# Two-level attention and a mixture of experts on one core: six of sixteen token tiles go to the experts by slots instead of through all eight

## The reference

```python
x = x + attention(layernorm(x))     # 16 heads of 8; window of 64 keys and four levels of pooled keys
h = layernorm(x)
gate = softmax(h @ Wg.T)            # 8 experts
val, idx = top_k(gate, 2); val /= val.sum() + 1e-9
for e in range(8):                  # 512 hidden columns: a, b = 256 each
    a, b = split(h @ W1[e].T + b1[e])
    out += ((a * sigmoid(b)) @ Wo.T + bo) * comb[..., e]
x = x + out
```

## Time and profile before

| | us |
|---|---|
| median of 3 runs | 288.18 |
| lowest and highest | 287.26, 295.06 |
| the profiled execution | 288.01 |
| its span | 286.2 |

### The profile page before, as it was taken

How to read it: one execution, slowest core, us unless ns; L and a number is a source line. 1 busy time by engine, 2 the same in 40 slices (tenths; PEclk the granted TensorE clock), 3 DMA queues, 4 the chain that set the end, 5 groups by cost and what they waited for, 6 DMA issues and landing times.

```text
span 286.2 us, 7298 instructions
## 1 busy us (share of the span) xinstructions
PE 273.4 (96%) x2705; PEld 226.5 (79%) x2705; DVE 154.6 (54%) x453; ACT 154.7 (54%) x316; POOL 135.8 (47%) x235
## 2 busy tenths in 40 slices
PE   7999999999999999993999999999999999999994
PEld 6868767887788988883888888788888678888883
DVE  7782644633344001322643162789886987777773
ACT  6765745534653432742487456544676555555551
POOL 7753302300041154140171301888885678888881
PEclk9999999989999975998999799999999999999999
DMA  7221176340097687558445011300000000000000
GB/s 212 61 58 60 57 171 192 81 126 2 11 289 277 168 229 170 145 155 165 128 144 154 26 22 21 85 10 10 10 11 9 10 11 10 9 11 18 11 9 19
DMA packets 19683, 24.14 MB, mean 84 GB/s; under 512 B 8312, under 2 KB 14456, under 8 KB 19648
## 3 DMA queue, kind: packets, MB, share of 16 engines
q1 hardware_dynamic: 18528, 22.80, 28.8%
q10 hardware_dynamic: 1120, 0.89, 1.2%
HBM read 11.91 MB, written 5.37 MB: 60 GB/s over the span
## 4 chain that ended last, share of the span: by engine, by line
PE 88%; DVE 3%; issue 3%; DMA 2%; SPq 1%; ACT 1%; POOL 1%; DVEq 0%; ACTq 0%; POOLq 0%
PE bank L1327 13%; PE bank L1140 12%; PE bank L1142 11%; PE bank L1141 11%; PE bank L1303 8%; PE bank L1306 6%; PE bank L1289 5%; PE bank L1221 3%; PE bank L1150 3%; PE bank L1331 2%; PE bank L1271 2%; PE bank L1237 2%; PE bank L1183 1%; DMA qst<-nshiftT 1%; PE bank L1171 1%
## 5 line engine op out<-in xcount | busy, mean ns | idle before, releaser
L752 POOL TENSOR_TENSOR work<-work 128x256 f32<-128x256 f32 x110 | 81.4, 744 | 31.2 <-DVE work L1123 18.3
L1123 DVE SCALAR_TENSOR_TENSOR work<-bank,comb,work 128x256 f32<-128x256 f32 x128 | 58.9, 480 | 24.7 <-ACT work L893 23.4
L893 ACT ACTIVATE work<-bank 128x256 f32<-128x256 f32 x128 | 48.4, 384 | 42.8 <-PE bank L1142 40.3
L868 ACT ACTIVATE work<-bank 128x512 f32<-128x512 f32 x64 | 37.7, 594 | 44.0 <-PE bank L1306 39.8
L1327 PE MATMUL bank<-work,vaug 128*64 128x64 f32 x1024 | 45.7, 235 | 0.0
L1327 PEld LDWEIGHTS bank<-work,vaug 128*64 128x64 f32 x1024 | 37.0, 144 | 9.0 <-issue 1.6
L658 POOL COPY vaug<-vwin 128x64 f32<-128x64 f32 x64 | 13.2, 250 | 51.7 <-PE bank L1331 51.5
L1303 PE MATMUL bank<-bar,ident_r 128*128 128x512 f32 x64 | 34.1, 533 | 0.0
L1306 PEld LDWEIGHTS bank<-qmk,kst 98*128 98x128 f32 x128 | 26.4, 206 | 4.3 <-issue 1.0
L1306 PE MATMUL bank<-qmk,kst 98*128 98x256 f32 x128 | 27.3, 297 | 0.0
L1141 PE MATMUL bank<-arena,xT_hi 128*128 128x512 f32 x64 | 25.1, 392 | 0.0
(11 more groups left out here) (217 smaller groups left out, 532.4 us busy)
## 6 DMA issues: line engine op xcount, KB each, us to landing
w_stage<-w SPq DMA_DIRECT2D x8, 512.0 KB, 3.9
qmk<-qst SPq DMA_DIRECT2D x20, 96.0 KB
qst<-arena SPq DMA_DIRECT2D x12, 128.0 KB, 3.8
kst<-arena SPq DMA_DIRECT2D x9, 128.0 KB, 3.2
qst<-q_rows SPq DMA_DIRECT2D x3, 384.0 KB, 4.2
qmk<-q_rows SPq DMA_DIRECT2D x12, 96.0 KB
p_rows<-kpool SPq DMA_DIRECT2D x2, 512.0 KB, 4.5
attT<-denom SPq DMA_DIRECT2D x8, 128.0 KB, 2.8
```

The lines of the kernel that those rows point to most:

```text
L752: gp.tensor_tensor(gacc[t % 2][:, :], gacc[t % 2][:, :], gtmp[(adds - 1) % TMP_RING][:, :], ALU.add).then_inc(acc_done, 1)
L868: act.activation(prob[lo % P_RING][:, :, :, :], bank[sc % SCORE_BANKS][:, :].rearrange("p (c j q) -> p c j q", c=2, j=GH), ACT.Exp).then_i ...
L893: act.activation(sig[hn % SIG_RING][:, :], bank[hn % HID_BANKS][:, HID:2 * HID], ACT.Sigmoid).then_inc(sig_done, 1)
L1123: dve.scalar_tensor_tensor(dst[:, :], bank[hn % HID_BANKS][:, 0:HID], comb[:, t, e:e + 1], sig[hn % SIG_RING][:, :], ALU.mult, ALU.mult).t ...
```

## The change

Tiles 0 and 1 of batch 0 and all of batch 1 keep all eight experts. Tiles 2 to 7 of batch 0 are routed. A step `rank` counts with small matmuls of the picks (against ones and a matrix of earlier tokens) how many picks of an expert stand before each token, and `route` makes from it, on DVE, for each token and each of its two picks the row of a slot (`slot_of`), and for each of 19 slot tiles of 128 rows the expert it belongs to (`expert_of`). Experts begin at multiples of 128 rows, which is why 12 x 128 picks take 19 tiles. POOL scatters the normalised rows to DRAM with 12 indirect DMAs in three steps, SP reads them back in five loads, PE transposes them (`slotsT`) and makes one unit of hidden work a slot, with the weights at an offset that is read into a register (`value_load`). The high parts of W1 are first moved side by side into `whi` by six DMAs. DVE multiplies without the gate value, SP writes the 128x256 results to DRAM, and POOL gathers two rows a token with two indirect DMAs a tile (`pull`); `hidT` of a routed tile is four matmuls against diagonal matrices of the gate values (`diag`), which add and transpose at once. For this the second norm and gate of batch 0 stand earlier, gate part 2 at the end of unit 6, and those of batch 1 stand beside the slots. SP also writes zeros to the slot rows at the start.

The core of the diff:

```diff
+DENSE = 2
+ROUTED = T // P - DENSE
+SLOT_TILES = (ROUTED * P * TOPK + E * (P - 1)) // P
...
-        5: {0: [("rden", 0)], 6: [("spread", 0, 0)], 7: [("spread", 0, 1), ("proj", 0, 0)], 8: [("proj", 0, 1)], 9: [("stat2", 0, 0)]},
+        4: {9: [("rden", 0)]},
+        5: {3: [("spread", 0, 0), ("spread", 0, 1), ("proj", 0, 0)], 4: [("proj", 0, 1)], 5: [("stat2", 0, 0)], 6: [("stat2", 0, 1)],
...
+        7: {0: [("rank",), ("route",)], 1: [("scatter", 0)], 3: [("gate", 0, 3), ("weigh",)], 4: [("scatter", 1)], 8: [("scatter", 2)]},
...
+        (0, 4): [("rden", 1)], (1, 5): [("hidT", 0)], (1, 6): [("spread", 1, 0), ("spread", 1, 1)], (1, 7): [("y", 0), ("proj", 1, 0)],
+        ("slot", 0): [("proj", 1, 1), ("stat2", 1, 0)], ("slot", 2): [("hidT", 1), ("stat2", 1, 1)], ("slot", 4): [("y", 1), ("apply2", 1, 0)],
...
+        ("slot", 15): [("gate", 1, 1)], ("slot", 17): [("gate", 1, 2), ("diag",)], ("slot", 18): [("gate", 1, 3)],
...
+            if e == 0 and r < TT:
+                s.append(("pull", r))
...
+                if u == NG:
+                    spill_reciprocals(0)
+                    load_reciprocals(0)
+                if u == UNITS - 1:
+                    sp.wait_ge(score_full, u * SPU)
+                    for n in range(6):
+                        sp.wait_ge(w1_ready, n + 1)
+                        move(whi[:, n, :], w1T_hi[n]).then_inc(whi_in, 16)
...
+            spill_reciprocals(1)
+            sp.wait_ge(slots_sent, 16 * TOPK * ROUTED)
+            sp.wait_ge(vaug_ready, 2 * UNITS)
+            for q in range(SLOT_GROUPS):
+                sp.dma_start(slot_rows[q], slots_dram[4 * q * P:min(4 * q + 4, SLOT_TILES) * P, :].rearrange("(i p) c -> p i c", p=P))\
+                  .then_inc(slots_in[q], 16)
             load_reciprocals(1)
...
+                    for n in range(*SCATTERS[step[1]:step[1] + 2]):
+                        r, k = n // TOPK, n % TOPK
+                        gp.indirect_dma_start(slots_dram, bass.IndirectOffsetOnAxis(ap=slot_of[:, k, r:r + 1], axis=0),
+                                              xnorm[:, DENSE + r, :], None).then_inc(slots_sent, 16)
...
+                    if r == 0:
+                        for i in range(OUT_RING):
+                            gp.wait_ge(hidden_sent[i], 16 * len(range(i, SLOT_TILES, OUT_RING)))
...
+                    for k in range(TOPK):
+                        gp.indirect_dma_start(pulled[r % 2][k], None, hidden_dram,
+                                              bass.IndirectOffsetOnAxis(ap=slot_of[:, k, r:r + 1], axis=0)).then_inc(pulled_in[r % 2], 16)
...
+                    pe.wait_ge(hid_done, hn - HID_BANKS + 1)
...
+                    mine = pe.value_load(expert_of[0:1, i:i + 1], min_val=0, max_val=E - 1)
+                    hi, lo = (w[:, bass.ds(mine, 1), :].rearrange("p o n -> p (o n)") for w in (whi, w1T_lo))
+                    ins = split3(bank[hn % HID_BANKS][:, :], tuple(x[i // 4][:, i % 4 * P:(i % 4 + 1) * P] for x in slotsT), (hi, lo))
```

256 lines of the change are left out of this document (205 added, 51 removed).

## The result

| | before | after |
|---|---|---|
| median of 4 runs each, side by side | 291.0 us | 317.92 us |
| lowest and highest | 287.26, 295.06 | 315.25, 328.25 |

The changed kernel takes 1.102 times as long (95% interval 1.083 to 1.121). That ratio, like those further down, is of the faster executions of each kernel, those that the clock slowed least; the quotient of the two medians is 1.092. The changed kernel is slower by 27 us, where 4.4 us less was forecast, and lies outside the range. Its profiled execution is the slowest of the four, 328.25 us (span 326.4).

What follows compares the result with a forecast made beforehand. PE was taken to set the experts' pace, with POOL 0.3 us a tile away. Terms -20.0 + 4.7 + 0.8 + 4.1 + 3.0 + 3.0 = -4.4 took 288.0 to 283.6 us; range 272 to 299.

Steps and rivals of the forecast that it cites:

- Units removed: Tiles 2 to 7 of batch 0: 19 slots replace 48 units, -20.0 us on PE, all on the chain.
- matmuls added: PE: slot transposes 2.1, six hidT steps 1.3 and rank's 12 small matmuls 1.3, together +4.7 us.
- Zeros, the six moves of W1 and earlier steps of batch 0: Start and attention stage: cost 0, the 4.58 us hole at batch 0's projection staying, give or take 1.
- Unit 7: End of attention: PE waits 0.8 us at rank; values behind scatters cost nothing at 0.75 us an issue, +3.4 at 1.28.
- g: Time one indirect DMA of 128 rows holds POOL: taken as 0.75 us, bounds 0.33 and 1.28.
- Reciprocals of batch 1: First projection of batch 1: their read lands late behind slot-row loads, a hole of +4.1 us (3.0 to 5.8).
- The slot stage: 19 slots beside batch 1's norm and gate: DVE sets the pace, 23.1 us against PE's 19.1, net +3.0.
- Register loads: Before each slot PE reads the expert's number: taken as 0; serial-loads rival 291 to 303 us, chance 0.17.
- Pulls: Tiles 8 to 13: two gathers a tile on POOL, 57.5 us against PE's 53.8, +3.0 after the ring's slack.
- POOL becomes the bound: Slower rival, six tiles with gathers: at 1.28 us an issue pulls cost 9.4, result 294.4 us, chance 0.25.
- DVE idle in a third of the experts' stage: Argument for the faster rival: DVE now idles 0.2 us before each multiply in the experts' stage.
- the covers: Faster rival: early reciprocals, PE's bank slack and short POOL issues hide most costs; -13.5, 274.5 us, chance 0.22.

Runs made afterwards that it cites:

- moves only: Kernel before with only batch 0's moved steps and two w1 steps placed as in the changed kernel, no routing; median 296.92 us beside 287.69.
- W1 first: Changed kernel with the last two W1 steps at the first place of unit 7, ahead of the scatters in POOL's order; median 326.46 us.
- constant expert: Routed kernel with reordered steps and idle matmuls, each slot's expert fixed at build, no register loads; median 311.85 us, 319.89 with loads.
- changed kernel again: Changed kernel rerun unedited for a second profile; median 328.39 us beside 287.69 of the kernel before.
- fillers: Changed kernel with idle TensorE matmuls ahead of four waits (both projections, rank, slot 0); median 320.95 us.
- later steps: W1 first with batch 0's chain from the projection on three score steps later; median 306.93 us, 19.5 less on the same chip.
- plain scatters: Routed kernel with reordered steps and idle matmuls, its twelve scatters made ordinary whole-tile transfers by SyncE; median 303.56 us beside 319.89 without that edit.

## Why the prediction was wrong

The forecast was 283.6 us, the result 317.9. By its steps:

- *Units removed, -20.0, and matmuls added, +4.7.* The first is right; the second was mis-sized. Rank's 12 matmuls are 24 in the trace, 5.1 us at the half clock they met, where 1.3 was priced. The four of a routed `hidT` are eight, 0.89 us (273.33 to 274.22 below) where 0.44 was priced, 2.7 us for six tiles.

```profile
273.33 1.13 PE L1424 MATMUL bank<-vpool,vaug 128*128 128x128 f32 x8 [0.51 <-DMA vaug<-hidden_rows,slot_of]
274.22 0.48 PE L1306 MATMUL bank<-wqkv_parts,kst 128*128 128x512 f32 x1
```

- *Zeros, the six moves of W1 and earlier steps of batch 0, "Cost 0".* **This step failed.** The moves alone cost 9 us by the medians (moves only, 296.9 against 287.7) and 7 by the means. The hole did not stay as long: it is 5.4 to 8.6 us in place of 4.58. What was overlooked besides is POOL's order: W1's subtraction came to stand behind `rstd` of the moved norm, so that ACT and then PE waited.
- *Unit 7.* The unknown g, the time an indirect DMA holds POOL, was taken at 0.75 us from SP's issues. It is 1.27, at the upper bound of 1.28 kept for the rival. The price given for that case, +3.4, named the values; what was late first was the two W1 steps, 5.0 us of full-clock time (W1 first).
- *Reciprocals of batch 1, +4.1.* Right: 4.19 us, ended by the spread. After it PE waited another 1.6 for DVE's part of the first slots.
- *The slot stage, +3.0.* At full clock 21.1 us, where the sum for DVE had 23.1; at the granted 0.76 it took 27.7.
- *Register loads, 0.* Right, shown by the constant expert. The floor of 600 ns that the Trainium skill gives (DMA: Bandwidth & Descriptors, latency and other measured facts) can't be seen in the time here. The queue of 64 ahead of TensorE that the Trainium skill gives (TensorE: Matmul & The Clock Gate, architectural detail) fits that, but no run shows its length.
- *Pulls, +3.0.* They cost 7.2 us. The rival "POOL becomes the bound" had 9.4 for g = 1.28 and a tile's pitch over 8; the pitch is 8.4.
- *DVE idle in a third of the experts' stage,* the argument for the covers, was misread: by the windows above DVE was busy for 83.9 of 112.4 us, so idle in a quarter.

With that rival's g the sum comes to 294.4, still 23 short, or 20 when the kernel before is taken at the 291.0 it had in the comparison. The larger error is in no single term: the sum priced every wait at its own length, and every matmul at full clock. The kernel before held the warning: behind the wait in the earlier trace rows its clock stood at half for some 3 us. The change made five waits of 1.6 to 6.7 us. In side-by-side runs its full-clock time is 8 us above the kernel before's and its clock loss 31.5 us above (changed kernel again; in its first four runs the loss was 32.6, against 11.0 to 16.6 of the kernel before on five chips). With no indirect transfer these are -1.5 and +26. That the clock loss makes up most of the time is shown. That waits lead to it is shown at the places that the fillers filled, and supported by later steps (20 less, same work) and plain scatters (12 less). It is not the whole cause. In six of the thirteen profiles of kernels with routing one stretch of half clock, 34 to 45 us long with TensorE busy, makes 17 to 22 us of the loss; the same wait stands ahead of it in profiles where the clock stayed up. How much one wait costs is not settled either: the same kernel lost 22 us on one chip and 35 on another, and the half clock behind a wait lasted from nothing to over 40 us. Which execution gets the long stretch, and why, stays open.

## What to carry to other kernels

Where the clock row falls behind waits, a new wait costs its length and can cost a stretch at half clock behind it, so a change that saves dense matmuls and adds waits can lose although its work is less: compare span times granted clock beside the times, and look for the waits first, in more than one profile. When steps are moved in a kernel whose engines follow one order, follow the orders of POOL and ACT too: what now stands behind a late result there holds up the next engine. Take an unknown issue time on GpSimd from nothing on SyncE's queue.
